# Two-layer graph network: a seventh group of two columns in the second layer, float32r type products

## The reference

```python
# layer 0
msg = einsum('ei,eio->eo', x[src], W_rel[type_90]) * e      # e: a score of source, edge and target
x = layernorm(x + segment_sum(msg, dst))
# layer 1
A = edge_emb[type_8].reshape(-1, 16, 16)
m = segment_sum(einsum('emh,eh->em', A, x[src]), dst)
x = layernorm(x + GRU(m, x))
```

## Time and profile before

| | |
|---|---|
| time, median of 3 runs | 5613.58 us (5613.08 to 5614.38) |
| the profiled execution | 5610.07 us |
| span in its profile | 5608.2 us |
| TensorE / its weight loads busy | 4950.1 us (88%) / 4647.6 us (83%) |
| VectorE busy | 4712.6 us (84%) |
| ScalarE busy | 4374.3 us (78%) |
| GpSimd busy | 4055.1 us (72%) |
| layer 0, its chunks | about 330 to 2815 us |
| layer 1, its chunks | 2978 to 5458 us |

### The profile page before, as it was taken

One profiled execution on the slowest core, in us unless ns is written; L12 is line 12 of the kernel. 1 busy time (PEld: TensorE's weight loads), 2 busy tenths in 40 slices (PEclk: granted clock), 3 DMA queues, 4 the chain that ended last, 5 costly groups with the idle time before them and its releaser, 6 DMA issues.

```text
span 5608.2 us, 106498 instructions
## 1 busy us (share of the span) xinstructions
PE 4950.1 (88%) x36141; PEld 4647.6 (83%) x36141; DVE 4712.6 (84%) x7893; ACT 4374.3 (78%) x5373; POOL 4055.1 (72%) x4261
## 2 busy tenths in 40 slices
PE   4597999999999999999948998999899899989974
PEld 1297999999999999999937888888888888888863
DVE  6589999999999999999936888888888888888864
ACT  5686888888888888888727888888888888888864
POOL 3376777777777777777766777777777777777766
PEclk8698999999999999999958999999999999999985
DMA  9811111111111111111121222222221122222221
GB/s 302 333 29 33 37 39 39 33 40 40 40 40 40 39 40 40 36 39 38 31 71 23 18 18 17 17 17 18 17 17 16 16 17 17 17 17 17 17 21 12
DMA packets 628151, 239.45 MB, mean 43 GB/s; under 512 B 520872, under 2 KB 601467, under 8 KB 627448
## 3 DMA queue, kind: packets, MB, share of 16 engines
q10 hardware_dynamic: 421742, 84.19, 8.6%
q0 software_dynamic: 136160, 39.20, 8.5%
q1 hardware_dynamic: 70186, 115.26, 6.0%
HBM read 72.97 MB, written 164.99 MB: 42 GB/s over the span
## 4 chain that ended last, share of the span: by engine, by line
DVE 45%; PE 30%; issue 13%; DMA 5%; POOL 3%; DVEq 1%; ACT 1%; ACTq 0%; SPq 0%; POOLq 0%
PE ps_table L717 26%; DVE work L1239 10%; DVE t_buf L1231 10%; DVE scanned L1197 9%; DVE t_buf L1243 8%; POOL sums L549 2%; DMA rows<-type_table,idx 2%; DVE rows L1246 2%; PE ps_table L727 1%; PE ps_misc L699 1%; DMA relation_table<-scanned 1%; DVE he_dot L1297 1%; DVE he_dot L1283 1%; POOL rows L549 1%; DMA relation_table<-t_buf 1%
## 5 line engine op out<-in xcount | busy, mean ns | idle before, releaser
L717 PE MATMUL ps_table<-node_halves,hot_key 128*128 128x320 f32 x24960 | 3910.1, 315 | 322.5 <-DVE t_buf L1231 307.8
L717 PEld LDWEIGHTS ps_table<-node_halves,hot_key 128*128 128x128 f32 x24960 | 3727.3, 191 | 389.3 <-DVE t_buf L1231 354.2
L888 ACT ACTIVATE hot_key<-ps_misc,less_key 128x512 fp32r<-128x512 f16 x3120 | 1874.7, 694 | 900.3 <-PE ps_misc L699 892.1
L549 POOL DMA_INDIRECT rows<-relation_table,idx x1976 | 1898.0, 961 | 660.7 <-issue 500.5
L549 POOL DMA_INDIRECT rows<-type_table,idx x1976 | 1866.7, 945 | 629.0 <-issue 515.5
L892 ACT ACTIVATE hot_key<-hot_key,ones 128x2560 fp32r<-128x2560 f32 x624 | 1520.5, 2437 | 20.3
L1231 DVE TENSOR_TENSOR t_buf<-ps_table,work 128x640 f32<-128x640 f32 x1248 | 1007.7, 811 | 199.3 <-PE ps_table L717 199.1
L1239 DVE TENSOR_REDUCE work<-t_buf 128x64 f32<-128x1280 f32 x624 | 927.3, 1486 | 21.4
L1243 DVE TENSOR_TENSOR t_buf<-ps_table,work 128x1024 f32<-128x1024 f32 x624 | 763.8, 1224 | 82.2 <-DVE work L1239 21.4
L1246 DVE TENSOR_REDUCE rows<-t_buf 128x64 f32<-128x1024 f32 x624 | 761.7, 1221 | 21.4
L727 PE MATMUL ps_table<-rel_mats,hot_type 90*128 90x256 bf16 x3744 | 463.8, 274 | 0.0
(11 more groups left out here) (206 smaller groups left out, 1624.8 us busy)
## 6 DMA issues: line engine op xcount, KB each, us to landing
scanned<-scanned ACTq DMA_DIRECT2D x52, 992.0 KB, 3.9
relation_table<-scanned SPq DMA_DIRECT2D x50, 765.0 KB, 6.6
relation_table<-t_buf SPq DMA_DIRECT2D x48, 765.0 KB, 6.6
rows<-relation_table,idx POOLq DMA_INDIRECT x1976
rows<-type_table,idx POOLq DMA_INDIRECT x1976
scanned<-scanned ACTq DMA_DIRECT2D x52, 496.0 KB
he<-in_edge_attr SPq DMA_DIRECT2D x48, 496.0 KB
type_table<-t_buf SPq DMA_DIRECT2D x14, 448.0 KB, 3.0
```

The lines of the kernel that those rows point to most:

```text
L549: pool.indirect_dma_start(out=rows[:, k, :], out_offset=None, in_=table, in_offset=bass.IndirectOffsetOnAxis(ap=index[:, k:k + 1], axis=0) ...
L717: last = pe.matmul(ps_banks[:, duo * DUO + t, 0:BLOCK_W], hot_key[:, b, g, edges], node_halves[:, half, g, :, :].rearrange("p f j -> p (f ...
L888: act.activation(hot_key[:, b, g, :], match_bank[:, 0, :], ACT.Abs, bias=less_key[:, g:g + 1])
```

## The change

Layer 0 keeps its six rounds of four columns (24 looked up, 38 gathered). Layer 1 gets a seventh round of two columns: 26 columns looked up, 36 gathered. The seventh round has 20 look-ups, 2 products, 4 transposes and one duo on VectorE. The keys of the next chunk move with `quads - 3` from round 3 to round 4 (counted from 0); nothing in `chunk_by_products` is reordered.

The type matrices become two float32r halves in place of three bf16 parts: layer 0 does 8 type products a round in place of 12, layer 1 still 4, from 64 partitions in place of 96. The type one-hots become float32r and a sixth block of the tile `hot`, so that one Relu covers all six blocks (3,072 values) in place of two (2,560 and 512); the Abs of the types runs on all 128 partitions. Splitting the matrices (a mask of the low 12 bits, a copy and a subtraction in place of two copies and two subtractions for three parts) takes VectorE fewer instructions, once in each layer, and one small load of `edge_emb` goes; these hunks are left out below.

```diff
--- before.py
+++ after.py
@@ -16,7 +16,7 @@
 EPS = 1e-5
 CHUNK = 62
 QUAD, DUO = 4, 2
-QUADS = (6, 6)
+GROUPS_OF = ((4, 4, 4, 4, 4, 4), (4, 4, 4, 4, 4, 4, 2))
 LEAD = 2
 
 
@@ -25,9 +25,10 @@
 
     def __init__(self, n, edge_types, kinds, strips, mats, rows):
         self.n, self.edge_types, self.kinds = n, edge_types, kinds
-        self.quads = QUADS[n]
+        self.groups = GROUPS_OF[n]
+        self.quads = len(self.groups)
         self.strips, self.mats, self.rows = strips, mats, rows
-        self.share = self.quads * QUAD
+        self.share = sum(self.groups)
         self.own = CHUNK - self.share
         self.duos = self.share // DUO
 
@@ -41,7 +42,7 @@
 
     def picks_done(self, m, q, duo):
 
-        return m * self.duos + (q * QUAD // DUO + duo + 1)
+        return m * self.duos + (q * (QUAD // DUO) + duo + 1)
 
     def quads_done(self, m, q):
 
...
@@ -152,17 +153,16 @@
         rel_stack = sb("rel_stack", [P, RW], BF16)
         he_w = sb("he_w", [P, D])
         rel_rows = sb("rel_rows", [RELS, D, D])
-        rel_mats = sb("rel_mats", [RELS, 3, D, D], BF16)
-        emb_sb = sb("emb_sb", [3 * STRIP, D * D])
-        type_mats = sb("type_mats", [3 * STRIP, D * D], BF16)
+        rel_mats = sb("rel_mats", [RELS, 2, D, D], F32R)
+        emb_sb = sb("emb_sb", [2 * STRIP, D * D])
+        type_mats = sb("type_mats", [2 * STRIP, D * D], F32R)
         ident_f16 = sb("ident_f16", [P, P], F16)
         less_key = sb("less_key", [P, BLOCKS])
         type_i = sb("type_i", [P, 1], I32)
         less_type = sb("less_type", [P, 2])
         match_i = sb("match_i", [P, 2, SHARE], I32)
         match_cols = sb("match_cols", [P, 2, 2, SHARE], F16)
-        hot_key = sb("hot_key", [P, 2, BLOCKS, QUAD * P], F32R)
-        hot_type = sb("hot_type", [P, 2, QUAD * P], BF16)
+        hot = sb("hot", [P, 2, BLOCKS + 1, QUAD * P], F32R)
 
         src_w = sb("src_w", [P, D])
         work_sizes = [2 * SHARE * BLOCK_TILES, SHARE * D, SHARE * D]
...
@@ -384,8 +384,8 @@
 
         layers = [
             Layer(0, types_sb, RELS, RELS,
-                  [rel_mats[:, k, :, :].rearrange("r o i -> r (o i)") for k in range(3)], rows0),
-            Layer(1, types_sb, TYPES, 3 * STRIP, [type_mats[:, :]], rows1),
+                  [rel_mats[:, k, :, :].rearrange("r o i -> r (o i)") for k in range(2)], rows0),
+            Layer(1, types_sb, TYPES, 2 * STRIP, [type_mats[:, :]], rows1),
         ]
 
         @block.sync
...
@@ -694,7 +694,7 @@
                 pe.wait_ge(keys_set[lay.n], m + 1)
                 wait_past(pe, match_sb[lay.n], m * lay.quads + q)
                 for k in range(2):
-                    for c in range(QUAD):
+                    for c in range(lay.groups[q]):
                         at = q * QUAD + c
                         last = pe.transpose(match_bank[:, k, c * P:(c + 1) * P],
                                             match_cols[:, parity, k, at:at + 1].to_broadcast([P, P]), ident_f16[:, :])
@@ -709,12 +709,13 @@
                         pe.wait_ge(t1_sb, GROUPS)
                 columns = [(t, slice((duo * DUO + t) * P, (duo * DUO + t + 1) * P)) for t in range(DUO)]
                 before = (m, q - 1) if q > 0 else (m - 1, lay.quads - 1)
-                wait_past(pe, picked_set[lay.n], lay.picks_done(*before, duo))
+                if q > 0 or duo * DUO < lay.groups[-1]:
+                    wait_past(pe, picked_set[lay.n], lay.picks_done(*before, duo))
                 b = lay.half(parity, q)
                 for t, edges in columns:
                     for g in range(BLOCKS):
                         for half in range(2):
-                            last = pe.matmul(ps_banks[:, duo * DUO + t, 0:BLOCK_W], hot_key[:, b, g, edges],
+                            last = pe.matmul(ps_banks[:, duo * DUO + t, 0:BLOCK_W], hot[:, b, g, edges],
                                              node_halves[:, half, g, :, :].rearrange("p f j -> p (f j)"),
                                              start=(g == 0 and half == 0), stop=(g == BLOCKS - 1 and half == 1))
                     last.then_inc(looked_up[lay.n], 1)
@@ -722,10 +723,10 @@
             def products(lay, m, parity, q):
                 wait_past(pe, products_used[lay.n], lay.quads_done(m, q - 1))
                 b = lay.half(parity, q)
-                for c in range(QUAD):
+                for c in range(lay.groups[q]):
                     for k, mats_part in enumerate(lay.mats):
                         last = pe.matmul(by_type[:, c, :, :].rearrange("p o i -> p (o i)"),
-                                         hot_type[0:lay.strips, b, c * P:(c + 1) * P],
+                                         hot[0:lay.strips, b, BLOCKS, c * P:(c + 1) * P],
                                          mats_part, start=(k == 0), stop=(k == len(lay.mats) - 1))
                 last.then_inc(products_ps[lay.n], 1)
 
@@ -736,7 +737,7 @@
                         spread_quad(lay, m, parity, q + 1)
                     elif not last:
                         spread_quad(lay, m + 1, 1 - parity, 0)
-                    for duo in range(QUAD // DUO):
+                    for duo in range(lay.groups[q] // DUO):
                         look_up(lay, m, parity, q, duo)
                     products(lay, m, parity, q)
 
@@ -879,18 +880,17 @@
             def one_hot(lay, m, parity, q):
 
                 quad = m * lay.quads + q
-                own = slice(0, lay.strips)
                 act.wait_ge(match_ps[lay.n], quad + 1)
                 wait_past(act, products_ps[lay.n], lay.quads_done(m, q - 2))
                 b = lay.half(parity, q)
-                types = hot_type[own, b, :]
+                edges = slice(0, lay.groups[q] * P)
                 for g in range(BLOCKS):
-                    act.activation(hot_key[:, b, g, :], match_bank[:, 0, :], ACT.Abs, bias=less_key[:, g:g + 1])
-                act.activation(types, match_bank[own, 1, :], ACT.Abs, bias=less_type[own, lay.n:lay.n + 1]
-                               ).then_inc(match_sb[lay.n], 1)
+                    act.activation(hot[:, b, g, edges], match_bank[:, 0, edges], ACT.Abs, bias=less_key[:, g:g + 1])
+                act.activation(hot[:, b, BLOCKS, edges], match_bank[:, 1, edges], ACT.Abs,
+                               bias=less_type[:, lay.n:lay.n + 1]).then_inc(match_sb[lay.n], 1)
                 act.wait_ge(match_sb[lay.n], quad + 1)
-                act.activation(hot_key[:, b, :, :], hot_key[:, b, :, :].bitcast(F32), ACT.Relu, bias=ones[:, 0:1], scale=-1.0)
-                act.activation(types, types, ACT.Relu, bias=ones[own, 0:1], scale=-1.0).then_inc(match_set[lay.n], 1)
+                act.activation(hot[:, b, :, edges], hot[:, b, :, edges].bitcast(F32), ACT.Relu, bias=ones[:, 0:1],
+                               scale=-1.0).then_inc(match_set[lay.n], 1)
 
             def chunks_out(lay, stored, scan_set, scan_out):
                 for q in range(1, lay.quads):
...
@@ -1223,9 +1221,11 @@
 
             def make_rows(lay, m, half, q, base, between):
 
-                for duo in range(QUAD // DUO):
+                size = lay.groups[q]
+                duos = size // DUO
+                for duo in range(duos):
                     own = q * QUAD + duo * DUO
-                    if duo == 1:
+                    if duo == duos - 1:
                         between(q)
                     dve.wait_ge(looked_up[lay.n], m * lay.share + (own + DUO))
                     dve.tensor_tensor(picked[:, duo * DUO:(duo + 1) * DUO, :, :],
@@ -1234,17 +1234,18 @@
                                       hot_tile[:, half, own:own + DUO, :].unsqueeze(2).to_broadcast(
                                           [P, DUO, D, BLOCK_TILES]), ALU.mult).then_inc(picked_set[lay.n], 1)
                 own = q * QUAD
-                sources = source[:, own:own + QUAD, :]
-                dve.wait_ge(picked_set[lay.n], lay.picks_done(m, q, 1))
-                dve.tensor_reduce(sources, picked[:, :, :, :], AX, ALU.add).then_inc(match_step[lay.n], 1)
+                sources = source[:, own:own + size, :]
+                dve.wait_ge(picked_set[lay.n], lay.picks_done(m, q, duos - 1))
+                dve.tensor_reduce(sources, picked[:, 0:size, :, :], AX, ALU.add).then_inc(match_step[lay.n], 1)
                 dve.wait_ge(match_step[lay.n], base + 1)
                 wait_past(dve, rows_made[lay.n], lay.quads_done(m, q - 1))
                 dve.wait_ge(products_ps[lay.n], lay.quads_done(m, q))
-                dve.tensor_tensor(by_in[:, :, :, :], by_type, sources.unsqueeze(2).to_broadcast([P, QUAD, D, D]),
+                dve.tensor_tensor(by_in[:, 0:size, :, :], by_type[:, 0:size, :, :],
+                                  sources.unsqueeze(2).to_broadcast([P, size, D, D]),
                                   ALU.mult).then_inc(products_used[lay.n], 1)
                 dve.wait_ge(products_used[lay.n], lay.quads_done(m, q))
```

(4 more changed lines are left out.)

39 lines of the change are left out of this document (18 added, 21 removed).

## The result

The changed kernel takes **5785.8 us** (median of 4, 5783.9 to 5786.9), the kernel before 5614.0 (median of 4): a ratio of 1.0308, 95% interval 1.0295 to 1.0321. It is slower, as forecast, but by 172 us where 82 were forecast, and above the range. The profiled execution has 5783.9.

A forecast was written before the change was run, and what follows sets the result against it. Layer 1 was taken as bound by its gathers, 47.46 us a chunk; after the change its rounds set 49.14, making layer 1 82 us longer: 5610.1 + 82, plus 3.5 for the median, 5696 us, range 5632 to 5745.

The forecast's parts named there:

- The keys' stall: Layer 1, VectorE making the next chunk's keys held TensorE 1.58 us; forecast to go, costing 0 to 1.6 if it stayed.
- the term of the type products in layer 1: Layer 1, TensorE: four float32r products forecast to take 0.08 us more a round, bounds 0 to 0.2.
- the round ahead: Layer 1, round 4, followed by four transposes in place of eight: forecast at 6.8 us.
- the clock: Layer 1, slow look-ups after TensorE's pause behind the seventh round: 1.1 us a chunk, bounds 0 to 1.5.
- The rival that the transposes keep the clock up: Layer 1: eight transposes in the pause keep the clock up, 57 us less, 5639 us; chance 0.17.
- the last chunk: End of layer 1, from its first look-up to the last gathered rows: forecast at 51.7 us.
- C: Layer 1: the seventh round is swallowed and the gathers set the period, 44.97 us a chunk, 5484 us; chance 0.04.
- B: Layer 1: products at 0.153 us and half the keys' stall left, 76 us more, 5770 us; chance 0.09.
- D: Layer 0 is not VectorE's alone and gains from the shorter products, 31 us less, 5665 us; chance 0.05.
- E: Both layers: float32r products at some multiple of the look-ups' time per column hold TensorE, over 5800 us; chance 0.03.

## Why the prediction was wrong

**Right.** The gathers go from bound to cover; VectorE's wait for rows is gone; layer 0 doesn't move (with 8 products a round in place of 12 TensorE waits 96.1 us in place of 39.2 from 1000 to 2500, 1.8 a chunk more where 1.4 were forecast). The float32r product on 90 partitions is 0.12 us:

```profile
1542.51 1.11 PE L728 MATMUL ps_table<-rel_mats,hot 90*128 90x256 f32 x8
1543.47 0.62 PE L699 MATMUL ps_misc<-ident_f,match_cols 128*128 128x128 f16 x8
```

0.96 / 8 = 0.120, against 0.122 in proportion to the look-ups, and the Relu has 2.86 for 2.87. The Trainium skill, "TensorE: Matmul & The Clock Gate", section "Weight-path perf modes — Fast Weight Load (FWL) and DoubleRow", keeps the fast weight load from FP32 inputs; whether or not it was at work in the kernel before, going without it did not bring the products to 0.153: by this row it costs at most 0.02 a product. The keys' stall went. The seventh round is set by ScalarE, 6.90 for 6.84, with the pause of 2.34 for 2.5.

**Wrong: the term of the type products in layer 1.** The forecast took 0.08 us a round (bounds 0 to 0.2) on the ground that operands and engine are those of the look-ups. The partitions are not: 64, where the look-ups have 128 and the products before had 96. The round came out at 7.13 and not 6.88: 5 x 0.25 = 1.25 us a chunk, and 0.11 more in round 4, two ahead of the seventh (6.91 for 6.8; the prediction calls it the round ahead). With that, TensorE's own path (6.04 + 0.66 + 0.43) became longer than ScalarE's, 6.82. The bound's upper end fell because it was taken from the price per column alone; the earlier trace rows could not show it, since all products there have 96 partitions. Nor was the price per column off: one more product costs 0.12 on 64 partitions too. What the sum had no term for is the loss at the two ends of the group.

**Wrong by a quarter: the clock.** 31 of 43 pauses in the earlier trace rows were followed by slow look-ups; after the seventh round it is 47 of 51, at a granted clock of 0.50. Why more often was not tried; the four exceptions stand 13 or 14 chunks apart, so it is no even chance at each pause. 47 / 51 x 1.53 = 1.4 us a chunk, 0.3 above the 1.1. The rival that the transposes keep the clock up is out: they lie in every pause.

The sum: 1.25 + 0.11 + 0.06 + 0.31 = 1.73 of the 1.80 us by which the mean chunk is longer than forecast (50.94 against 49.14); 51 x 1.80 = 92 of the 95 us of the miss. The other 3 lie in the last chunk, 5628.10 - 5572.86 = 55.2 us for 51.7.

**The rivals.** C fell with the fixed order: the earlier spread, with a buffer of its own for the small group, brings the seventh round from 6.90 to 5.45 at the least; VectorE's wait keeps it from the 3.8. B's total (5770) came near for a wrong reason: no keys' stall, and products slow by their partitions, not by the column. D holds only under stops. E had the right part, the products, and the wrong mechanism: no multiple of the time per column, but a loss once a group, in layer 1 alone.

The two causes of the miss are seen round by round, not in an undisturbed whole time; how the 92 us divide between them rests on the sum above.

## What to carry to other kernels

A small group at the end of a cycle is no small round where another engine prepares the next full one: price it at that engine's latency, add what the clock takes after the pause, and issue the next round's inputs before it. Then count the pauses and slow starts again: here the earlier issue shortened the round, but left most of the slow starts. When a stage is packed into fewer partitions, look for a row with that number of partitions before taking the price per column from its neighbours; here padding 64 rows to 96 with zeros took 0.26 us off a round. A gain on the bound resource ends at the next one, so ask for the period of the rounds without it, and for the one after that.

## What the runs showed of the hardware

Matmuls on 64 partitions between others on 128: their first weight load started 0.19 us after the end of the load before it, as the last look-up was ending, in both types, and in bfloat16 the next load on 128 waited again (0.21). The float32r round lost 0.26 us by it; one more product in the group cost 0.12 us as elsewhere. On 96 partitions the full rounds had neither loss; the float32r loads of the seventh round, behind 20 look-ups, came late there as well in 50 of 52 chunks (0.3 us after the last look-up's load, for 0.15), so the number of partitions is not the only condition, and the others were not looked for. A pause of 2.34 us behind a short one of 0.3 to 0.5 was followed by look-ups that began at the lower of the clock's two levels (1.2 and 2.4 GHz) in 47 of 51 chunks (granted clock 0.50 over the first 3 us), 1.5 us lost each time; 16 small matmuls in the pause, 2 us of work, kept it at the upper one in most chunks (1 of 47 slow), even with a rest of 0.16 to 0.6 us ahead of the look-ups. With the earlier spread the pause was shorter, at times 1.03 us, and 31 of 46 starts were slow all the same.
